# Attention: where ScalarE copies the turned probabilities of the odd units

## The reference

```python
h = 16; d = 16; s = 8; m = n // s                    # 16 heads of 16, 8 segments of 64 rows
q = rotary(split_heads(x @ Wq)) * d ** (-0.5)
kv = rotary(split_heads(x @ Wkv))                    # keys and values are the same tensor
lsim = einsum('csmd,csnd->csmn', qs[:, 1:], concat(kvs[:, :-1], kvs[:, 1:]))
attn1 = softmax(where(causal, mask_value, lsim))     # a segment sees itself and the one before
out1 = merge_heads(einsum('csij,csjd->csid', attn1, kvs_ccs)) @ Wo + bo
# the first segment sees only itself and has its own Wo0, bo0
```

## Time and profile before

| | |
|---|---|
| median of 3 runs | 2365.93 us (2363.47 to 2369.75) |
| profiled execution | 2368.05 us |
| its span | 2366.3 us |
| TensorE busy | 1824.5 us (77%) |
| VectorE busy | 2117.0 us (89%) |
| ScalarE busy | 1656.0 us (70%) |
| GpSimd busy | 956.6 us (40%) |
| attention | about 45 to 484 us of the span |

### The profile page before, as it was taken

One profiled execution on the slowest core, in us unless ns is written; L12 is line 12 of the kernel. 1 busy time (PEld: TensorE's weight loads), 2 busy tenths in 40 slices (PEclk: granted clock), 3 DMA queues, 4 the chain that ended last, 5 costly groups with the idle time before them and its releaser, 6 DMA issues.

```text
span 2366.3 us, 47628 instructions
## 1 busy us (share of the span) xinstructions
PE 1824.5 (77%) x12321; PEld 1478.2 (62%) x12321; DVE 2117.0 (89%) x9102; ACT 1656.0 (70%) x5481; POOL 956.6 (40%) x1608
## 2 busy tenths in 40 slices
PE   5888888788888777877777788877877877343887
PEld 3555555455587666777777777777766777342654
DVE  6888777679817999999999999999999999999887
ACT  4878888667746666667777777777777666555776
POOL 0000000001005666666665666666666555666110
PEclk8999899889997888788888777888778777666999
DMA  6000000000000000000000000000000000000001
GB/s 189 18 18 22 18 18 18 13 1 1 1 1 1 1 1 1 1 1 1 2 1 1 1 1 2 1 1 1 1 1 1 1 1 1 1 1 1 10 28 36
DMA packets 14351, 25.00 MB, mean 11 GB/s; under 512 B 1280, under 2 KB 12032, under 8 KB 13824
## 3 DMA queue, kind: packets, MB, share of 16 engines
q1 hardware_dynamic: 14080, 21.97, 3.2%
HBM read 12.27 MB, written 4.19 MB: 7 GB/s over the span
## 4 chain that ended last, share of the span: by engine, by line
DVE 63%; PE 14%; issue 13%; ACT 5%; POOL 0%; DVEq 0%; POOLq 0%; ACTq 0%
DVE xs L1581 9%; DVE pn L1561 8%; DVE bank L1565 8%; DVE U L1630 7%; DVE bank L1595 7%; DVE pn L1586 6%; DVE kv L1619 5%; PE bank L282 3%; PE bank L267 3%; ACT prob L923 2%; PE bank L585 2%; DVE bank L1603 2%; DVE bank L1615 1%; PE bank L632 1%; PE bank L669 1%
## 5 line engine op out<-in xcount | busy, mean ns | idle before, releaser
L750 PE MATMUL bank<-U,ident 128*128 128x128 f32 x2048 | 463.5, 398 | 159.6 <-ACT go L1064 140.1
L750 PEld LDWEIGHTS bank<-U,ident 128*128 128x128 f32 x2048 | 430.1, 257 | 195.5 <-issue 162.3
L1779 POOL TENSOR_TENSOR wu<-U,stg 128x256 f32<-128x256 f32 x512 | 317.7, 620 | 561.3 <-DVE U L1630 561.3
L1253 ACT ACTIVATE xs<-U 128x128 f32<-128x128 f32 x1024 | 261.4, 301 | 304.1 <-DVE U L1630 301.4
L761 PE MATMUL bank<-stack,tm 128*128 128x64 f32 x1792 | 273.8, 324 | 110.1 <-ACT tm L994 100.4
L761 PEld LDWEIGHTS bank<-stack,tm 128*128 128x128 f32 x1792 | 263.7, 237 | 127.5 <-ACT tm L994 115.8
L1708 POOL TENSOR_TENSOR kv<-stg 128x256 f32<-128x256 f32 x513 | 317.4, 619 | 0.0
L1581 DVE TENSOR_TENSOR xs<-U,bank 128x128 f32<-128x128 f32 x1024 | 243.5, 278 | 62.1 <-ACT bank L1107 61.1
L1565 DVE TENSOR_TENSOR bank<-wu,bank 128x128 f32<-128x128 f32 x1024 | 290.0, 283 | 1.8 <-POOL wu L1779 1.4
L735 PE MATMUL bank<-wcat,yT 128*128 128x224 f32 x1024 | 275.9, 425 | 5.8 <-issue 5.4
L1595 DVE TENSOR_TENSOR bank<-pn,bank 128x128 f32<-128x128 f32 x1024 | 248.3, 288 | 1.1 <-issue 0.8
(11 more groups left out here) (213 smaller groups left out, 3708.0 us busy)
## 6 DMA issues: line engine op xcount, KB each, us to landing
out_x<-x SPq DMA_DIRECT2D x8, 512.0 KB, 2.9
x<-in_x SPq DMA_DIRECT2D x1, 3584.0 KB, 16.9
Vs<-V SPq DMA_DIRECT2D x8, 384.0 KB, 4.6
Vs<-V SPq DMA_DIRECT2D x8, 288.0 KB, 3.3
lane<-in_lanes SPq DMA_DIRECT2D x8, 256.0 KB, 3.2
wcat<-in_wcat SPq DMA_DIRECT2D x1, 1792.0 KB, 14.5
wraw<-in_w_up SPq DMA_DIRECT2D x1, 1024.0 KB, 19.0
wraw<-in_w_down SPq DMA_DIRECT2D x1, 1024.0 KB, 11.4
```

The costliest lines, as they stand in the source:

```text
L750: last = pe.matmul(rsum.rearrange("p (t i) -> p t i", i=HD), ident[:, :], steps[:, :, :, j], start=(j == 0), stop=(j == HD - 1))
L1779: pool.tensor_tensor(ij(wu[:, :]), ij(U[:, half if j else 1 - half, (j - 1) % STEPS, :]), col(stg[:, half, j, TW, :]), ALU.mult).then_inc( ...
```

## The change

In `units` of ScalarE, the copy of the turned probabilities of an odd unit t is called in step t+2 instead of step t+1. In step t+1 ScalarE now goes straight to the exponentials of unit t+1; in step t+2 it does the copy of unit t and then the exponentials of unit t+2. What else a step has keeps its place, so what the loop puts between the exponentials of t+1 and the units of step t+2 now comes before the copy. The number of instructions and all waits within them are the same.

```diff
             def units(b, w, n):
 
-                if 1 <= w <= n and w % 2 == 0:
-                    copy_probs(b, w - 1)
+                if 2 <= w <= n + 1 and w % 2 == 1:
+                    copy_probs(b, w - 2)
                 if w < n:
                     exponentials(b, w)
```

## The result

| | before | changed |
|---|---|---|
| median, us (runs) | 2366.23 (4) | 2393.86 (4) |
| lowest to highest | 2363.47 to 2369.75 | 2392.55 to 2394.73 |
| ratio | 1 | 1.0108, interval 1.009 to 1.0126 |
| profiled execution, span | 2366.3 | 2390.8 |
| mean granted clock | 0.836 | 0.828 |

The change makes the kernel slower by 1.1%, 27.6 us by the medians. Forecast were 21.7 us and 2388.

The account below looks back on a forecast made before the run. Attention was taken as bound by the order in which three in-order engines hand units over. 7 x (1.9 + 0.1 + 1.2) less 0.75 gave +21.7 us; 2368.05 + 21.7 - 2.1 = 2388, own range 2381 to 2394, wider range 2370 to 2398.

Parts of the forecast that it names:

- the stall: Step 13: TensorE held 2.2 us for a late copy, of which 1.9 us per batch carried into the next batch.
- weigh(11): TensorE's product of unit 11's probabilities with the values (L647), forecast to start at 363.55 instead of 361.32.
- copy(11): ScalarE's copy of unit 11's turned probabilities (L932), forecast to start at 362.81, behind the split and kT copies.
- exp(14): ScalarE's exponentials of unit 14 (L923), forecast 1.4 us later, at 367.13 against 365.75.
- exp(15): ScalarE's exponentials of unit 15 (L923), forecast 1.9 us later, at 370.44 against 368.56.
- the wait that would show it: A new wait of L647 for L932, 30 to 40 us in all, longest about 2.2 on unit 11.
- The last batch: The batch with no next one to prepare, forecast 0.75 us shorter, once, as ScalarE waits less before unit 4's exponentials.
- turn(3): TensorE's turning of unit 3's probabilities (L632); in the last batch ScalarE waits 0.75 us before copying that unit.
- weigh(5): TensorE's product of unit 5's probabilities with the values, behind step 6's split: forecast 0.1 to 0.2 us late, 0.1 added.
- the clock: One more slow-clock stretch per batch on the projection behind step 13's stall: 1.2 us, range 0.7 to 1.7, seven times.
- the term of the order: The loss per batch from later copies without the clock: 1.9 us from step 13 plus 0.1 from step 6.
- The stages behind cost nothing more: The feed-forward and retention stages after the attention keep their order and add 0 us.

Follow-up runs that it names:

- both fillers: The changed kernel with four, then two, extra matmuls without use on TensorE in step 13 of each batch but the last: ratios 1.0069 and 1.0041.

## Why the prediction was right, and where its terms were off

- **Right, the stall.** weigh(11) held for copy(11): forecast 2.2 us, shown by its own wait in the kernel with that copy alone moved (2.08 idle) and by the loss coming and going with that one unit (1.0105, 0.9979) and with ready work put in its place (1.0004). By itself it puts exp(14) 1.3 later (forecast 1.4). In the two batches at full clock, 51.6 and 54.6, it makes weigh(11) 2.2 later beyond what step 7 had already cost, exp(14) 1.3, exp(15) 1.8 (1.9), and the next batch 1.8 (1.9).
- **Right, the wait that would show it.** 38.1 us of L647 for L932 (30 to 40), the longest 1.8 on the matmuls and 2.2 on their weight loads, batches of 58.0 (57 to 58) at 0.91 (0.91). The last batch is 1.2 us shorter from turn(3) to its end (42.1 us before, 40.9 after); the forecast was 0.75, and 0.77 of it is there at turn(4) (2.74 to 1.97 us). In the other profiles of the two kernels it takes 42.7 to 44.3 and 40.8 to 40.9.
- **Mis-sized, weigh(5): 0.1 forecast, 1.2 measured.** I read the row of step 7 in batches in which TensorE was at half clock there: turn(6) took 0.91 to 1.11 us and the projecting out of step 6 up to 1.98, and both hid the copy. The changed kernel mostly has the full clock at that place and then waits 1.17: in its three profiles that is so in 18 of 21 batches, and in the other three, which had the half clock in step 6, the wait is 0.14 at most. With the half microsecond that copy(13) and its like cost at odd units, the order without copy(11) costs 2.0 a batch at full clock (53.31 against 51.35), where the forecast's terms come to 0.6. A wait that is covered by slow matmuls is not covered when they run fast.
- **Nearly right, the clock: +1.2 forecast, +0.9 measured** against the batch of 54.1, but not as told. I added one slow stretch on step 13's projection. It is there, begins before the stall, lasts 6.8 us and costs 2.0; the stretch that lay on step 6 now lies on step 7's projection, and that of steps 17 and 18 is gone. Against the mean of the kernel before, 54.3 a batch, which holds more slow clock than 54.1, the net is some 0.6. That it is near the forecast is partly luck. That idle TensorE keeps the projection slow is shown by both fillers: with more matmuls it is at 1.98 in all seven batches, and the time is less. What sets off the slow clock at turn(12), and why the other stretches moved, stays open. The Trainium skill's remark ("TensorE: Matmul & The Clock Gate", What's actually happening) is that for modelling the ramp penalty is under one per cent of a typical kernel's span. This stage does not bear it out as a reason to leave the term away: the slow clock costs 3.4 of 58.0 us here, and seven times that is 24 us, by itself 1.0% of the kernel.
- **Sum.** 3.0 + 0.9 = 3.9 a batch against 3.2. The means over the profiles, 58.1 and 54.3, differ by 3.8, so by 26.5 in seven batches; the last batch gives back 2.1 (43.0 to 40.9), and the means of the attention in the table, 458.3 against 434.1, differ by 24. Single pairs of profiles differ by 19 to 28. The medians differ by 27.6, of which some 3 are not traced to a stage. So the time of 2394, at the upper edge of my own range of 2381 to 2394, was reached with the term of the order too small (2.0 for 3.0 to 3.3) and that of the clock too large (1.2 for 0.6 to 0.9).
- **"The stages behind cost nothing more"** holds for the change, as far as seven profiles show, but one execution can differ by 5 us there.

## What to carry to other kernels

Moving work out of the way of one engine moves it closer to whoever waits for its result: before it is moved, add up everything that the program issues between the old place and the new one, in the step where most is between, and look at what the waiting engine has queued behind the wait. One unit in eight was enough for the whole loss here, and a call one line lower, directly behind the exponentials, made a small gain. An in-order engine's total of waits says little; a wait in front of ready work of the engine that leads is the one that costs. And "no slower" does not mean that the new order is free: with all copies moved but one, a batch was 2.0 us longer at equal clock, and more granted clock hid it. Compare stretches at the same granted clock before putting a price on an order.

## What the runs showed of the hardware

- At full clock a batch of this attention takes 51.6 us, against 54.1 with 6.8 us at half clock in it (1.0 and 0.94 granted) and the same instructions.
- Adding two matmuls without use to each batch made the changed kernel faster, from 1.0108 to 1.0041 of the kernel before, by filling a wait of some 2 us (2.08 idle where copy(11) alone was moved), behind which the projection then took 1.98 us and not 3.6 to 3.8.
- What a slow stretch costs depends on where it falls. With all copies moved but copy(11), two batches with 3.4 us at half clock in step 6 took 53.3 and 53.5 us, as long as the one at full clock (53.3); TensorE did not wait for copy(5) in them, where it waits 1.17 in the others. One with 3.3 us in step 4 took 54.6.
- A stage far behind the change in which TensorE is the busiest engine (68 to 77 us) took 80 to 81 or 85 to 86 us in the same code, at 0.83 to 0.85 or 0.76 to 0.78 of the clock. Two kernels are not compared by one profile each where such a stage is in them.
